# Reordering the first loads and the preparation of tables in a per-item adapter with layer norm

## The reference

```python
# x (128, 128, 512) f32: B items, S rows of H; ids (128,) int32; 10 languages L
# W1 (L, 512, 128), b1 (L, 128), W2 (L, 128, 512), b2, gamma, beta (L, 512), all f32
w1 = W1[language_ids]
w2 = W2[language_ids]
h = jnp.einsum('bsh,bha->bsa', hidden_states, w1) + b1[language_ids][:, None, :]
h = jax.nn.relu(h)
adapted = jnp.einsum('bsa,bah->bsh', h, w2) + b2[language_ids][:, None, :]
x = hidden_states + adapted
mean = jnp.mean(x, axis=-1, keepdims=True)
var = jnp.mean(jnp.square(x - mean), axis=-1, keepdims=True)
normed = (x - mean) * jax.lax.rsqrt(var + LN_EPS)
adapter = normed * gamma[language_ids][:, None, :] + beta[language_ids][:, None, :]
return hidden_states + adapter
```

## Time and profile before

| | us |
|---|---|
| median of 3 runs (lowest to highest) | 318.31 (317.29 to 318.52) |
| profiled execution | 316.75 |
| its span in the trace | 315.0 |
| mean granted clock of TensorE in it | 0.974 |
| busy share of the span: TensorE, VectorE, ScalarE, GpSimd | 92%, 92%, 83%, 59% |

### The profile page before, as it was taken

The page is one execution under the profiler, slowest core; times in us unless marked ns, Lnnn a source line. Parts: engine busy times, 40 slices in busy tenths (PEclk is TensorE's granted clock), DMA queues, the critical chain, the costliest instruction groups (busy, mean ns, idle before and its releaser), DMA issues.

```text
span 315.0 us, 7506 instructions
## 1 busy us (share of the span) xinstructions
PE 289.5 (92%) x2008; PEld 253.8 (81%) x2039; DVE 289.8 (92%) x621; ACT 263.0 (83%) x601; POOL 186.2 (59%) x217
## 2 busy tenths in 40 slices
PE   1757959999999999999999999999999999999972
PEld 1237758889998888998888998888999888999861
DVE  5998856999999999999999999999999999999996
ACT  3977438889988889899989988999989988988872
POOL 2960742666655666565566665656656566665562
PEclk9968779999999999999999999999999999999998
DMA  5999999899999999899898989999898889885324
GB/s 155 332 389 372 293 331 390 276 340 352 358 347 328 321 313 302 302 318 318 292 315 313 299 309 310 318 302 311 290 319 311 315 304 311 286 291 202 116 110 177
DMA packets 56441, 94.03 MB, mean 298 GB/s; under 512 B 3387, under 2 KB 14711, under 8 KB 56273
## 3 DMA queue, kind: packets, MB, share of 16 engines
q1 hardware_dynamic: 56302, 93.41, 87.4%
q10 hardware_dynamic: 99, 0.14, 0.1%
HBM read 44.78 MB, written 33.55 MB: 249 GB/s over the span
## 4 chain that ended last, share of the span: by engine, by line
PE 79%; SPq 10%; issue 3%; DMA 3%; DVE 2%; DVEq 1%; ACT 0%
PE ps_h L504 33%; PE ps_y L525 28%; PE ps_T L488 16%; SPq L287 5%; DMA x_io<-in_x 2%; PE ps_h L497 2%; SPq L269 2%; SPq L257 1%; SPq L282 1%; DVE ps_y L663 1%; DVE ps_y L644 1%; SPq L172 1%; SPq L250 1%; DVEq L172 1%; DMA ids_raw<-in_itok_B 1%
## 5 line engine op out<-in xcount | busy, mean ns | idle before, releaser
L358 POOL TENSOR_TENSOR x_io<-x_io,beta_all 128x512 f32<-128x512 f32 x128 | 163.0, 1284 | 37.3 <-DVE ps_y L644 27.9
L504 PE MATMUL ps_h<-x_T,w_stage 128*128 128x128 f32 x1024 | 126.2, 277 | 0.0
L504 PEld LDWEIGHTS ps_h<-x_T,w_stage 128*128 128x128 f32 x1024 | 121.0, 194 | 0.8
L421 ACT ACTIVATE cut<-ps_y,row_sum 128x512 bf16<-128x512 f32 x128 | 87.9, 687 | 16.3 <-PE ps_y L525 11.4
L676 DVE SCALAR_TENSOR_TENSOR x_io<-ps_y,rstd,x_io 128x512 f32<-128x512 f32 x128 | 90.2, 747 | 2.6 <-DVE rstd L668 0.3
L663 DVE SCALAR_TENSOR_TENSOR ps_y<-ps_y,neg_mean,gamma_all 128x512 f32<-128x512 f32 x128 | 90.3, 750 | 1.7 <-ACT cut L421 1.7
L488 PE MATMUL ps_T<-identity,x_io 128*128 128x128 f32 x512 | 69.4, 280 | 11.2 <-DMA x_io<-in_x 10.1
L488 PEld LDWEIGHTS ps_T<-identity,x_io 128*128 128x128 f32 x512 | 62.2, 145 | 20.8 <-issue 12.6
L401 ACT COPY x_T<-ps_T 128x1024 f32<-128x1024 f32 x64 | 63.5, 992 | 6.7 <-PE ps_T L488 6.5
L525 PE MATMUL ps_y<-w_high,h_high 128*128 x128 | 62.3, 486 | 3.9 <-DVE w_low L625 2.2
L644 DVE SCALAR_TENSOR_TENSOR ps_y<-x_io,b_all 128x512 f32<-128x512 f32 x93 | 62.9, 704 | 0.0
(11 more groups left out here) (67 smaller groups left out, 150.9 us busy)
## 6 DMA issues: line engine op xcount, KB each, us to landing
x_io<-in_x SPq DMA_DIRECT2D x64, 512.0 KB, 5.1
out<-x_io SPq DMA_DIRECT2D x63, 512.0 KB, 3.9
w_stage<-w_all SPq DMA_DIRECT2D x58, 256.0 KB, 3.3
w_stage<-in_L_cond_W SPq DMA_DIRECT2D x12, 256.0 KB, 6.5
x_io<-in_L_cond_W SPq DMA_DIRECT2D x5, 512.0 KB, 7.8
b_all<-in_L_cond_b SPq DMA_DIRECT2D x1, 2560.0 KB, 14.3
w_all<-in_L_cond_W SPq DMA_DIRECT2D x5, 512.0 KB, 7.2
out<-x_io SPq DMA_DIRECT2D x2, 256.0 KB, 2.0
```

The costliest lines, as they stand in the source:

```text
L358: nc.gpsimd.tensor_tensor(x_slot(t), x_slot(t), of_lang(beta_all, lang), ALU.add).then_inc(x_beta_ready, 1)
L421: nc.scalar.activation(squares[:, t % 2, :], ps_y[t % Y_BANKS][:, :], ACT.Square, scale=-float(H), bias=stat(row_sum, t), accum_out=stat(s ...
L504: last = nc.tensor.matmul(bank[:, b * S:(b + 1) * S], w1_stage[:, 2 * (p % STAGE_PAIRS) + b, c, :], x_T[:, (2 * p + b) % 4, c, :], start=F ...
```

## The change

- *Loads.* SP's order becomes: ids, gamma, x of pair 0, W2 chunks 0 and 1, W1 of pair 0, W2 2 to 4, x and W1 of pairs 1 to 3, x of 4; then, behind a wait for the parts of b1, b2, beta and gamma, `b2_all`, and the W1 table's parts among W1 of 4, x of 5, x of 6, W1 of 5, x of 7; its last part is in the loop. ScalarE's three small loads go ahead of its table load, that of beta first.
- *Slots and stores.* 24 slots of x instead of 20; SP's loop loads x of p+8 and stores p-3 (`STORE_LAG`).
- *W1.* Pairs 0 to 8 (before: 0 to 5) are staged from HBM, and in runs of 2 KB (`w1_runs`); row 4q + c of W1 goes to partition q, so the transposes of these pairs take every fourth column of x. `copy_w1` is one step later.
- *Tables.* gamma and beta are cut in two parts (an fp32r one and the rest) over 20 partitions, in one fp32r table that lies in `w2_low`; the matmul that spreads them takes `signed_pick`, broadcast, in place of `pick`. Small rows lie in `b2_all` until it is loaded. b1 is cut by POOL. b2 is centred by VectorE (`centre_b2`), between the first two means of W2.
- *First two pairs.* VectorE seeds the bank with x alone (`seed_x`), and PE adds b2 in `second_product`, as for ScalarE's tiles.
- *Order.* ScalarE does `high_w2(2)` ahead of `copy_x(1)`, VectorE's list is rearranged, and PE's first two pairs stand ahead of its loop.

```diff
-SLOTS = 20
+SLOTS = 24
...
-STAGE_HBM = 6
+STAGE_HBM = 9
 FIRST = 2
 EARLY = 2
+STORE_LAG = 3
...
+    w1_runs = w1.rearrange("l (p c) a -> p l c a", c=C)
...
+        table_parts = w2_low[:, L - 2:L, :]
+        rounded = b2_all[0:2 * L, 0:2, :].bitcast(F32R)
+        gamma_rows = b2_all[0:2 * L, 2, :]
+        beta_rows = b2_all[0:2 * L, 3, :]
...
+        def without_b2(t):
+            return by_scalar(t) or t < 2 * EARLY
...
+            sp.dma_start(gamma_rows, gamma.unsqueeze(0).broadcast_to([2, L, H])).then_inc(s_gamma_rows, 16)
...
+                table = w1_runs if q < STAGE_HBM else w1_all
+                for b in range(2 if q < STAGE_HBM else 1):
...
+            def load_w1(n):
+                langs = slice(n * LC, (n + 1) * LC)
+                sp.dma_start(w1_all[:, langs, :, :], w1_rows[:, langs, :, :]).then_inc(s_w1, 16)
+
+            def load_x_behind_w2(p):
+                sp.wait_ge(w2_low_ready, (p - X_FIRST + 1) * LC)
+                load_x(p)
+
+            def store(p):
+                sp.wait_ge(out_ready, 2 * p + 2)
+                sp.dma_start(out_pairs[:, p, :, :], x_pair_slots(p)).then_inc(stored[p % X_PAIRS], 16)
+
+            load_x(0)
+            load_w2(0)
+            load_w2(1)
...
             stage_w1(0)
...
             for n in range(2, W_CHUNKS):
                 load_w2(n)
...
+            for p in range(1, 4):
+                load_x(p)
+                stage_w1(p)
+            load_x(4)
+            sp.wait_ge(b1_parts_ready, 1)
+            sp.wait_ge(b2_parts_ready, 1)
+            sp.wait_ge(beta_parts_ready, 1)
+            sp.wait_ge(gamma_parts_ready, 1)
             sp.dma_start(b2_all[:, :, :], b2.partition_broadcast(128)).then_inc(s_b2, 16)
...
+            load_w1(0)
+            stage_w1(4)
+            load_w1(1)
+            load_x(5)
+            load_w1(2)
+            load_x(6)
+            stage_w1(5)
+            load_w1(3)
+            load_x_behind_w2(X_FIRST)
+
+            for p in range(PAIRS - 1 + STORE_LAG):
                 if p + STAGE_AHEAD < PAIRS:
                     stage_w1(p + STAGE_AHEAD)
...
+                if p == 0:
+                    load_w1(4)
+                ahead = p + X_FIRST + 1
+                if ahead < X_PAIRS:
+                    load_x_behind_w2(ahead)
+                elif ahead < PAIRS:
+                    sp.wait_ge(stored[ahead % X_PAIRS], x_loads(ahead - X_PAIRS))
+                    load_x(ahead)
+                if p >= STORE_LAG:
+                    store(p - STORE_LAG)
...
+            nc.gpsimd.tensor_scalar(part_sign[:, :], later_part[:, 0:1], 2.0, -1.0, ALU.mult, ALU.add)\
+                .then_inc(part_sign_ready, 1)
+            pool.wait_ge(part_sign_ready, 1)
+            nc.gpsimd.tensor_scalar(signed_pick[:, :], pick_row[:, :], part_sign[:, 0:1], None, ALU.mult)\
+                .then_inc(pick_ready, 1)
...
+            pool.wait_ge(parts_zero, 4)
+            nc.gpsimd.tensor_copy(rounded[:, 1, :], beta_rows).then_inc(pool_cut_step, 1)
+            pool.wait_ge(pool_cut_step, 1)
+            nc.gpsimd.tensor_scalar(beta_rows, beta_rows, later_part[0:2 * L, 0:1], None, ALU.mult).then_inc(pool_cut_step, 1)
+            pool.wait_ge(pool_cut_step, 2)
+            nc.gpsimd.tensor_tensor(table_parts[0:2 * L, 1, :], beta_rows, rounded[:, 1, :].bitcast(F32), ALU.subtract)\
+                .then_inc(beta_parts_ready, 1)
+            pool.wait_ge(s_b1_rows, 16)
+            cut_in_three(b1_rows, b1_cut, b1_parts[0:3 * L, :], 2, b1_parts_ready)
             pool.wait_ge(b2_centred, 1)
-            cut_in_three(b2_rows[:, :], b2_cut[:, 1, :], parts[0:3 * L, 2 * H:3 * H], 4, b2_parts_ready)
+            cut_in_three(b2_rows, b2_cut, b2_parts[0:3 * L, :], 6, b2_parts_ready)
...
+            act.dma_start(beta_rows,
+                          beta.unsqueeze(0).broadcast_to([2, L, H])).then_inc(s_beta_rows, 16)
+            act.dma_start(b1_rows,
+                          b1.unsqueeze(0).broadcast_to([3, L, A])).then_inc(s_b1_rows, 16)
+            act.dma_start(b2_rows,
+                          b2.unsqueeze(0).broadcast_to([3, L, H])).then_inc(s_b2_rows, 16)
             act.wait_ge(set_ready, 4)
             nc.scalar.activation(table_load[:, :], eps[:, :], ACT.Sqrt, bias=eps[:, 0:1])
...
-            nc.scalar.copy(pick[:, :, :], pick_row[:, :].unsqueeze(2).broadcast_to([128, L, 128])).then_inc(pick_ready, 1)
...
+                if STAGE_HBM <= p + 2 < PAIRS:
+                    copy_w1(p + 2)
...
+            high_w2(2)
             copy_x(1)
-            high_w2(2)
+            high_w2(3)
             high_h(0)
-            high_w2(3)
             copy_x(2)
+            high_w2(4)
             high_h(1)
-            high_w2(4)
...
+                rows_of = "s (p c) -> s c p" if t // 2 < STAGE_HBM else "s (c p) -> s c p"
+                columns = x_slot(t).rearrange(rows_of, c=C)
...
+                    last = nc.tensor.transpose(ps_T[:, t % 2, c, :], columns[:, c, :], identity[:, :])
...
-                if by_scalar(t):
-                    nc.tensor.matmul(bank, is_lang[:, t:t + 1].broadcast_to([128, S]), parts[:, 2 * H:3 * H],
+                if without_b2(t):
+                    nc.tensor.matmul(bank, is_lang[:, t:t + 1].broadcast_to([128, S]), b2_parts[:, :],
                                      start=False, stop=False, skip_group_check=True)
...
+                nc.tensor.matmul(spread_bank(n), signed_pick[:, n % L:n % L + 1].broadcast_to([128, 128]),
+                                 table_parts[:, n // L, :], start=True, stop=True).then_inc(spread, 1)
...
+            for p in range(FIRST):
+                first_half(p)
+            pe.wait_ge(ids_ready, 1)
+            langs = {p: langs_of(pe, p) for p in range(FIRST)}
+            pe.wait_ge(b2_parts_ready, 1)
+            pe.wait_ge(w2_low_ready, L)
+            for p in range(FIRST, PAIRS):
+                n = p - FIRST
+                for b in range(2):
+                    second_product(2 * n + b, langs[n][b])
+                first_half(p)
+                langs[p] = langs_of(pe, p)
...
+            nc.vector.memset(zero[:, :], 0.0).then_inc(zero_ready, 1)
+            dve.wait_ge(zero_ready, 1)
+            nc.vector.tensor_copy(table_parts, zero[:, :].unsqueeze(2).broadcast_to([128, 2, H])).then_inc(parts_zero, 1)
             nc.vector.memset(b1_parts[:, :], 0.0).then_inc(parts_zero, 1)
+            nc.vector.memset(b2_parts[:, :], 0.0).then_inc(parts_zero, 1)
...
+            dve.wait_ge(s_gamma_rows, 16)
+            nc.vector.tensor_copy(rounded[:, 0, :], gamma_rows).then_inc(cut_step, 1)
+            dve.wait_ge(cut_step, 1)
             dve.wait_ge(later_part_ready, 1)
-            dve.wait_ge(s_gamma_rows, 16)
-            cut_in_three(x_io[0:3 * L, 2 * ROWS_PAIR, :], cut[0:3 * L, 0, :], parts[0:3 * L, 0:H], 0, gamma_parts_ready)
-            dve.wait_ge(s_b1_rows, 16)
-            cut_in_three(b1_rows[:, :], cut[0:3 * L, 1, 0:A], b1_parts[0:3 * L, :], 4, b1_parts_ready)
+            nc.vector.scalar_tensor_tensor(table_parts[0:2 * L, 0, :], gamma_rows, later_part[0:2 * L, 0:1],
+                                           rounded[:, 0, :].bitcast(F32), ALU.mult, ALU.subtract).then_inc(gamma_parts_ready, 1)
...
+            def seed_x(n):
...
+                    nc.vector.scalar_tensor_tensor(ps_y[t % Y_BANKS][:, :], x_slot(t), 1.0, x_slot(t), ALU.mult, ALU.max,
...
+            def centre_b2():
+
+                dve.wait_ge(s_b2_rows, 16)
+                nc.vector.reduce_sum(b2_sum[:, :], b2_rows, axis=mybir.AxisListType.X).then_inc(b2_summed, 1)
+                dve.wait_ge(b2_summed, 1)
+                nc.vector.tensor_scalar(b2_neg_mean[:, :], b2_sum[:, :], -1.0 / H, None, ALU.mult).then_inc(b2_mean_ready, 1)
+                dve.wait_ge(b2_mean_ready, 1)
+                nc.vector.tensor_scalar(b2_rows, b2_rows, b2_neg_mean[:, 0:1], None, ALU.add)\
+                    .then_inc(b2_centred, 1)
+
+            mean_of_w2(0)
+            centre_b2()
+            mean_of_w2(1)
+            mean_of_w2(2)
             for n in by_dve:
                 dve.wait_ge(spread, n + 1)
                 nc.vector.tensor_copy(spread_to(n), spread_bank(n)).then_inc(spread_dve, 1)
-            for n in range(W2_AHEAD):
-                low_w2(n)
-            mean_of_w2(2)
+            low_w2(0)
             mean_of_w2(3)
+            low_w2(1)
+            mean_of_w2(4)
             low_w2(2)
-            mean_of_w2(4)
+            dve.wait_ge(spread_act, len(by_act))
+            dve.wait_ge(spread_dve, len(by_dve))
+            seed_x(0)
+            low_w2(3)
             low_h(0)
-            low_w2(3)
-            seed_early(0)
             low_w2(4)
+            low_h(1)
+            seed_x(1)
             dve.wait_ge(ids_ready, 1)
             langs = {n: langs_of(dve, n) for n in range(2)}
```

(57 more changed lines are left out.)

91 lines of the change are left out of this document (5 added, 86 removed).

## The result

The changed kernel takes **362.37 us** (median of 4 runs, 361.93 to 365.31) against 318.03 before (4 runs, 317.29 to 318.52): ratio 1.143, 95% interval 1.139 to 1.148. Forecast were 311.6 (308.9 to 316.2). The profiled execution took 362.32, its span is 360.6, its granted clock 0.974, the same as before.

A forecast was written before the change was run, and what follows sets the result against it. PE was taken as the bound from 50 to 290 us, in steps of 4.29; an earlier beginning brings T(4) from 47.2 to 40.5, and that gain of 6.7 off the median of 318.31 gives 311.6 us (308.9 to 316.2).

The forecast's parts named there:

- Edits at nothing: Main loop: 24 slots, stores three pairs later and the later W1 copy cost 0 beside a never idle PE.
- Rival E: Main loop: stores bunched with loads make W1 or x late; 2.6 us per hundredth; 2% same, 2% slower.
- copy_x of pair 0: ScalarE's opening: with centring and the copy of pick gone, it starts at 8.6 instead of 10.18.
- First reduction of W2: VectorE's opening: W2's first chunk, directly behind x of pair 0, is there at 8.7 instead of 11.96.
- T(4): Start of PE's step 4: 40.5 instead of 47.2, gain 6.7; afterwards only pace and drain count, 267.8 us.
- T(2): Start of PE's step 2 (second products of pair 0, transposes of 3, first products of 2): 29.3, gain 2.9.
- late bound: If W2's first chunk came no earlier than before: T(2) at 32.1, T(4) at 43.3, a gain of 3.9.
- Centring on VectorE: VectorE's opening: centring b2, moved from ScalarE where it took 1.6, takes 1.3, between 0.9 and 2.
- POOL's cuts of b2: POOL's opening: the cuts start at about 11.3 and end at 18.1, before 14.36 to 21.16.
- The cold step: T(2) to T(3): PE idles and the slow step repeats, 5.76 + 0.8 for b2 matmuls, T(3) = 35.9.
- Rival C: Transposes of pairs 3 to 8 slowed by 16-byte step: 1.5 times, 315.1, 8%; twice, no change, 4%; fourfold, 333, 4%.
- Rivals B and D: B: DMA engines become the wait, 316.0, 10%. D: another wait takes T(2) or the first scaling, 315, 8%.

The follow-up runs named there:

- lag2: The changed kernel with STORE_LAG 2 instead of 3, nothing else: 328.08 us.
- load_later: The changed kernel, lag 3 kept, with each turn of SP's loop loading x of p+7 in place of p+8: 326.04 us.
- lag2_store_first: The changed kernel with STORE_LAG 2 instead of 3 and the store issued ahead of the wait and the load of x: 312.93 us.
- store_first: The changed kernel, lag 3 kept, with SP issuing the store ahead of the wait and the load of x: 313.31 us.
- held_512: held_lag2 with W1 of the first nine pairs in 512-byte runs and transposes without a step: 311.40 us.
- held_lag2: lag2_store_first with GpSimd's loop held back until W2 is ready: 310.50 us.

## Why the prediction was wrong

**The step that failed** is "Edits at nothing: 24 slots, stores three pairs later ... lie beside a PE that is never idle". I priced the later store by asking which engine covers it, and not by the loop in which it stands. Three facts were at hand and were never put together. The diff puts the store behind the wait and the load. The store waited for, p-4, is the one that the turn before issued. And the 24 slots give no room, since x is also loaded into the slot that has just been given up. The page of before lists the store's landing:

```profile
out<-x_io SPq DMA_DIRECT2D x63, 512.0 KB, 3.9
```

3.9 us, and the 0.42 between the load's issue and the store's, are 4.3: the pace itself, with no room for any growth; measured were 4.92. SP's waits of before show that the landing was already felt there, 10.4 of these 11.9 us before 100 us:

```profile
SPq L250 <- DMA out<-x_io: 11.9, 12, 7.0
```

The price of this term was 0; it was 51.7 us.

**Rival E** came nearest ("The pace itself moves", "stores bunched with loads"), at 4% in all and each hundredth of a step at 2.6 us. A turn of 5.34 is 24 hundredths over 4.29, 64 us at that price; it was 51.7, because only 52 turns wait. Its mechanism was half of it. Bunching did not overload the engines, whose share fell from 0.91 to 0.74; but with a load of x issued 0.42 us ahead of it the store landed in 4.9 us instead of 3.9, and at 3.9 the turn would have been the pace. The longer landing alone does not make the cycle: in lag2 and load_later stores landed in 5.6 and 5.7 us, and SP's loop waited for them 0.5 us in all and not at all. The loss needs the serial wait, which a rival of contention cannot see.

**The terms of the beginning**, one by one. copy_x of pair 0: 8.45, forecast 8.6. First reduction of W2: 8.04, forecast 8.7. This term varies: with the same opening list of transfers it was 8.62 in load_later and 8.80 in lag2_store_first, with T(4) at 41.01 and 40.73, but 10.98 in store_first and 10.95 in lag2, with T(2) at 32.6 and 32.5 and T(4) at 44.08 and 43.62, near the forecast's late bound (32.1 and 43.3). Centring on VectorE: 9.57 to 10.93, 1.36, forecast 1.3. POOL's cuts of b2 ended at 17.38, forecast 18.1; `b2_all` landed 13.6 after its issue at 17.45, at 31.1, ahead of the first scaling at 32.65. T(2) 30.15, forecast 29.3: high_w2(4) ended at 28.15, as forecast, and the 0.9 is the last low_w2, 2.47 for 1.41, slowed beside POOL (1.41 or 1.42 in each of the four kernels that hold GpSimd's loop back); I had taken off slowing where POOL ends sooner and not seen that POOL's loop now begins sooner too. The cold step: T(3) 36.48, 6.33 after T(2), forecast 5.76 + 0.8 = 6.56. Then 4.63, forecast 4.63.

**Rival C**, strided transposes. The timeline after has one of the pairs with the step, and then the first without:

```profile
42.60 1.12 PE L512 MATMUL ps_T<-identity,x_io 128*128 128x128 f32 x8
...
60.09 1.03 PE L512 MATMUL ps_T<-identity,x_io 128*128 128x128 f32 x8
```

0.09 us for eight, 8% of a transpose, 0.5 us in all over six pairs. In held_512, where no transpose has the step, the eight start 0.87 us ahead of what follows them, and 0.95 in the changed kernel: the step is the cause. The rule of the Trainium skill, SBUF — State Buffer (Door 1: The DMA port swizzle), by which an access that goes to a new 16-byte line each time pays a penalty, agrees in sign with this row. It doesn't give the size; here the penalty neither doubled nor quadrupled the price.

**Rivals B and D** did not come: x of pair 8 was there, with no wait for x between 45 and 60 us, and `b2_all` was in time. With the serial turn mended and the store ahead of x, the changed kernel takes 313.3 (store_first) or 312.9 (lag2_store_first), both in the range forecast and 1.3 to 1.7 us above 311.6: the rest of the sum held.

## What to carry to other kernels

When a diff moves an instruction in a queue that issues transfers, write down one turn of its loop with every wait, and follow each wait to the turn in which its transfer was issued. If the next store stands behind a wait for the last one's landing, the turn can't be shorter than that landing, however idle the DMA engines are; put the issue that others will wait for ahead of the wait. An engine that is never idle hides the work of others, but not a cycle through a queue that it depends on. And when one late transfer is moved up, look at the next in the same queue before its wait is counted as a gain.

## What the runs showed of the hardware that was not expected

- A register load of two values from SBUF by TensorE's queue took from 0.53 to 2.5 us (100 to 290 us of each trace), with medians of 0.54 in the changed kernel (DMA share 0.74), 1.34 before, 1.41 in store_first, 1.89 in load_later and 1.98 in lag2 (share 0.90 to 0.92 in these four). In load_later and lag2, where the median passed its cover of 16 matmuls, the kernel took 13 to 15 us more than in store_first. A load of four values, every second step, had a median of 0.34. The Trainium skill, DMA: Bandwidth & Descriptors (Latency and other measured facts), gives about 600 ns as the floor of a `tensor_load`, which I take to be this instruction; TensorE's shortest here were 0.53 us for two values and 0.33 for four, so these traces disagree with it.
- The order of three transfers issued within 2 us by one queue, with the same bytes and the same room, was worth 15 us (lag2 against lag2_store_first). A store issued ahead of the load of x landed in a median of 4.1 to 4.2 us (lag2_store_first, store_first), one issued behind it in 5.6 to 5.7 (lag2, load_later).
- A GpSimd addition of 128x512 beside a VectorE instruction on two rows of W2 made the latter 2.47 (changed kernel) or 3.09 us long (store_first) instead of 1.41. In the kernel before, the addition began at 31.41, when the second of VectorE's two instructions was already running: these took 1.41 and the additions 3.02, where two beside held_lag2's took 2.50.
- The time of the first W2 chunk's landing (the start of its reduction) varied from 8.0 to 11.0 us between the changed kernel and store_first, whose opening lists of transfers are the same.
